# Graph kernel: three quarters of each source one-hot made by a compare and a multiply, with two numbers per partition

## The reference

```python
x = x + filter(h, src, dst)          # three hops of sums over edges, by node degrees
x = x + gat(h, edge_index, ...)      # attention over the edges, softmax by dst
x = x + relational(h, ..., edge_type, edge_weight, W1..W3)   # three rounds
x = x + attention(h, edge_attr_64, ...)
```

```python
scaled = feat * d_invsqrt
agg = segment_sum(scaled[src], dst, num_segments=3125)
```

## Time and profile before

| | |
|---|---|
| median of 3 runs | 6393.17 us (6391.6 to 6401.1) |
| profiled execution, its own time | 6387.14 us |
| its span, first to last instruction | 6385.3 us |
| PE busy | 4142.3 us, 65% |
| DVE busy | 3184.7 us, 50% |
| POOL busy | 3315.9 us, 52% |
| scatter, line 440 | 784 transfers, 874.8 us busy |
| hot_src, line 901 | 245 instructions, 263.5 us busy |
| hot_dst, line 903 | 245 instructions, 60.3 us busy |
| matmuls of the counting, line 975 | 1715, 385.0 us busy |

### The profile page before, as it was taken

One profiled execution on the slowest core, in us unless ns is written; L12 is line 12 of the kernel. 1 busy time (PEld: TensorE's weight loads), 2 busy tenths in 40 slices (PEclk: granted clock), 3 DMA queues, 4 the chain that ended last, 5 costly groups with the idle time before them and its releaser, 6 DMA issues. The chain is left out here.

```text
span 6385.3 us, 88933 instructions
## 1 busy us (share of the span) xinstructions
PE 4142.3 (65%) x19143; PEld 2771.2 (43%) x19144; DVE 3184.7 (50%) x7069; ACT 793.1 (12%) x2439; POOL 3315.9 (52%) x3323
## 2 busy tenths in 40 slices
PE   6969970003899788778746668888888844444431
PEld 5844430001499744444435534445445433333331
DVE  6966650005899456565566761122122255545556
ACT  1210000000110022222220010010010012222210
POOL 0048887772000077777733006737747547777761
PEclk7569985556899889898979979989999865555555
DMA  4311120001367577777745546767677643333331
GB/s 121 102 56 32 42 53 2 2 2 58 136 239 263 174 199 216 209 216 214 216 139 163 153 155 239 238 226 251 228 237 244 196 132 81 81 82 82 81 85 52
DMA packets 516122, 909.59 MB, mean 142 GB/s; under 512 B 100755, under 2 KB 349832, under 8 KB 476628
## 3 DMA queue, kind: packets, MB, share of 16 engines
q1 hardware_dynamic: 410094, 741.27, 35.7%
q0 software_dynamic: 105824, 165.90, 11.4%
HBM read 680.21 MB, written 226.65 MB: 142 GB/s over the span
## 5 line engine op out<-in xcount | busy, mean ns | idle before, releaser
L2768 POOL DMA_INDIRECT l_gathered<-l_table,l_st x816 | 775.6, 951 | 855.3 <-issue 782.0
L440 POOL DMA_INDIRECT by_src<-src_rec,src_pos x784 | 874.8, 1116 | 560.0 <-ACT attr_turned L742 321.2
L1790 POOL DMA_INDIRECT l_edges_by_src<-l_by_src,l_edges_st x816 | 786.7, 964 | 727.3 <-SPq L1884 478.9
L1790 POOL DMA_INDIRECT l_edges_by_src<-l_q,l_edges_st x816 | 778.4, 954 | 347.4 <-issue 242.9
L2837 PE MATMUL psum<-l_blocks,l_rows 128*128 128x512 f32 (+1 forms) x2016 | 814.7, 565 | 2.3 <-ACT l_rows L2779 2.3
L1869 PE MATMUL psum<-l_rows,l_edges_hot_t 128*128 x1632 | 443.1, 453 | 565.9 <-DVE l_scores L2907 542.6
L1688 PE MATMUL psum<-pair_hot_weight,pair_hot_dst 128*128 128x512 f32 x1200 | 642.9, 678 | 176.4 <-DVE pair_hot_dst L1678 165.6
L2796 DVE TENSOR_SCALAR l_hot<-iota,l_loc,l_weight 128x128 f32<-128x128 f32 x816 | 223.0, 360 | 916.8 <-PE psum L2853 913.6
L1869 PEld LDWEIGHTS psum<-l_rows,l_edges_hot_t 128*128 128x128 f32 x1632 | 379.0, 330 | 634.3 <-issue 634.3
L2837 PEld LDWEIGHTS psum<-l_blocks,l_rows 128*128 128x128 f32 x2016 | 373.5, 199 | 417.1 <-issue 412.3
L2504 PE MATMUL psum<-l_scaled,l_counts 128*128 128x128 f32 x3750 | 424.2, 277 | 18.8 <-ACT l_scaled L2429 18.8
(11 more groups left out here) (483 smaller groups left out, 5454.8 us busy)
## 6 DMA issues: line engine op xcount, KB each, us to landing
l_blocks<-pair_blocks SPq DMA_DIRECT2D x216, 1024.0 KB, 5.2
l_counts<-counts SPq DMA_DIRECT2D x65, 1600.0 KB, 6.8
pair_blocks<-pair_block SPq DMA_DIRECT2D x75, 1024.0 KB
l_edges_loc<-loc_by_tile SPq DMA_DIRECT2D x416, 128.0 KB, 3.0
l_rows<-l_edges_by_src SPq DMA_DIRECT2D x204, 256.0 KB
l_sum_rows<-l_rows SPq DMA_DIRECT2D x204, 256.0 KB, 2.6
attr_then_counts<-in_edge_attr SPq DMA_DIRECT2D x14, 1568.0 KB
counts<-attr_then_counts SPq DMA_DIRECT2D x13, 1600.0 KB
```

Of the source, the lines that this page charges most:

```text
L440: pool.indirect_dma_start(table, bass.IndirectOffsetOnAxis(ap=pos[:, e:e + 1], axis=0), rec[:, e, :], None).then_inc(s_out[g % R], 16)
L1790: pool.indirect_dma_start(a[:, r, g, :], None, table_src, bass.IndirectOffsetOnAxis(ap=st[:, r, g:g + 1], axis=0))\
L2768: pool.indirect_dma_start(sent[:, p, g, :], None, by_type, bass.IndirectOffsetOnAxis(ap=st[:, p, g:g + 1], axis=0))\
```

## The change

In `one_hots` the one instruction that wrote 3200 columns of `hot_src` becomes two. The first writes columns 0 to 2431 (19 of the 25 windows) by `is_equal` with the source number and then `mult` with a second number per partition, which is a column of ones. The second writes the other 768 columns by `is_equal` alone, as before. What stands in `hot_src` is the same. `hot_dst` is as it was. Each of the three instructions adds one to `s_hot`, so PE waits for three a visit.

```diff
+    WEIGHED = 19 * P
...
-            v.tensor_scalar(hot_src[:, bass.ds(place, 1), 0:NP].rearrange("p a c -> p (a c)"), iota[:, :],
-                            shifted[:, 0, bass.ds(t, 1)], None, ALU.is_equal).then_inc(s_hot, 1)
+            for cols, one in ((slice(0, WEIGHED), k.ones[:, 0:1]), (slice(WEIGHED, NP), None)):
+                v.tensor_scalar(hot_src[:, bass.ds(place, 1), cols].rearrange("p a c -> p (a c)"), iota[:, cols],
+                                shifted[:, 0, bass.ds(t, 1)], one, ALU.is_equal,
+                                *((ALU.mult,) if one is not None else ())).then_inc(s_hot, 1)
...
-                    pe.wait_ge(s_hot, (t + b) * 2 + 2)
+                    pe.wait_ge(s_hot, (t + b) * 3 + 3)
```

## The result

The changed kernel takes 6327.56 us (median of 4 runs, 6321.92 to 6332.13) against 6394.44 us for the kernel before (median of 4 runs, beside it). The ratio is 0.9894, with a 95% interval of 0.9876 to 0.9911: about 67 us faster. The forecast was 6313, with a range of 6270 to 6341 that also takes in the rival case two.

A forecast was written before the change was run, and what follows sets the result against it. POOL's scatter was taken to end the block, with the counting 560 us to spare. Missing scatters fall from 98 to 39 (quick 2, middle 9, slow 28), 74 us off 6387.1: 6313, own range 6295 to 6341, wider range 6270 to 6341.

The forecast's parts named there:

- case two: Two-number hot_src runs slower and leaves POOL alone: 6285 us at slow rate (chance 0.25), 6277 at half rate (0.10).
- The ceiling of 122 to 124 us: Scatter on POOL beside the counting: 97 transfers missing, 122 us lost, 124 over the whole line; the most that can be won.
- The rate of the two-number instruction: hot_src on DVE: 0.263 ns a column kept, so 0.91 us for 2432 columns and 0.41 for 768; other bound 1.04 ns.
- four: Two-number hot_src at half rate, 1.56 us, holds POOL out throughout: 40 more scatters missing, 6437 us; chance 0.12.
- Case three: Short holds catch the scatters that the long one lets go; rhythms stay, nothing moves: 6387 us; chance 0.10.
- The two requests and the holds: Each scatter asks twice, 0.46 to 0.71 us apart; an earlier end of the long hold lets the second request slip through.
- middle rhythm: hot_src starts 1.3 to 1.6 us apart; a scatter takes two visits, 2.74 us; change makes it one; missing 53 to 9.
- What I credited to the second number: Its extra 59 ns on hot_src delays the next long hold's start to 1.61 us, letting the second request through.
- The sum: Scatters missing over quick, middle and slow rhythms: 39 instead of 98, so 74 us less, 6313 us.
- quick: Window's start, hot_src starts 1.12 to 1.14 us apart, two visits a scatter; becomes one visit of 1.31; missing 17 to 2.
- slow rhythm: hot_src starts 1.6 to 1.7 us apart, one scatter a visit before and after; missing 28, unchanged.
- a mere shift: Everything behind the block should only be shifted in time.

The follow-up runs named there:

- the gap in the iota: Kernel before with the iota kept as 25 rows of 128 with a gap of two, hot_src still one uncut one-number instruction: 6268.66 us, ratio 0.9801.
- the summing compare: Changed kernel with the 2432 columns written by a one-number compare that also sums its answers, 768 by plain compare: 6274.9 us, ratio 0.981.
- the moved cuts: One-number split of hot_src cut elsewhere, against before: 1664 + 1536 columns 6311.11 us; 2816 + 384 6370.69 us; 3072 + 128 6398.47 us.
- the uncut kernel: All 3200 columns of hot_src in one two-number compare and multiply, against the kernel before: 6404.62 us, ratio 1.0004.
- the halves: hot_src in two plain one-number compares of 1664 and 1536 columns, against the kernel before: 6311.11 us, ratio 0.9869.
- the two kernels without holds: Long hot_src in a form that doesn't hold POOL out: gapped iota rows, 6268.66 us; 2432 columns by compare with sum, 6274.9 us.

## Why the prediction was right

**What bounds.** In the two profiled executions the block's end moved by exactly what the last scatter moved by, 66.1 us, with DVE idle for 504 us ahead of it. The ceiling of 122 to 124 us was right: the two kernels whose long instruction doesn't hold POOL out win 121 and 123 us at the last scatter.

**The rate of the two-number instruction.** Forecast 0.91 and 0.41 us at 0.263 ns a column, with four times that as the other bound. Measured 0.92 (median, 0.905 the least) and 0.410. Both rival cases two and four needed a slower rate, and fell with it. Case three, in which nothing moves, fell by the 361 scatters where there had been 310. As ideas the lower rates were sound: case two, with no hold, is what the gap in the iota and the summing compare made on purpose, at 6269 and 6275 us where it had said 6277 and 6285. Its price had a slip: 379.7 + 999 is 1379, not 1382. And its condition that PE might stay at 1.2 GHz did not come true: between 419 and 1302 us, where the summing compare sets the pace, the granted clock was 0.95 of full speed.

**The two requests and the holds.** Right in mechanism: one scatter a visit in the middle rhythm, 2.4 us scatters gone, and the time between the long hold's end and the next one decides, as the moved cuts show. I placed the second request between 0.46 and 0.71 us after the first; scatter by scatter it comes at 0.46 to 0.49, at the short end of that, so that the cut at 19 windows had about 0.06 us to spare with one number and 0.11 with two (a distance of 0.40 against 0.34 and 0.28).

**What I credited to the second number was wrong in weight.** The prediction let the extra 59 ns move the next hold's start and counted on it for the margin (1.61 against 1.52). The later start is there: the boundary lies 0.06 us lower with two numbers. But in the uncut kernel the instruction also ends 0.06 later, and the two cancel; in the cut one it is room that is not needed, since the split without the second number does as well. The forecast's total did not depend on it.

**The sum.** Forecast 39 scatters missing, last one near 1419, 6313 us. Measured 46, 1427.1 and 6327.6. Here are the terms, with the scatters that start between one long hot_src and the next, by how far apart these start:

| starts of hot_src apart | before: visits, missing | forecast missing | after: visits, missing |
|---|---|---|---|
| up to 1.60 us (quick and middle) | 132, 65 | 11 | 153, 16 |
| 1.60 to 1.70 (slow) | 89, 24 | 28 | 68, 22 |
| longer (changes of window, and others) | 24, 9 | nothing | 24, 8 |

Two terms were too small. The forecast kept the quick and middle rhythms at 1.31 and 1.37 us a visit, as though the counting stayed hidden behind PE. That step failed in part: 132 visits of the changed kernel last 1.35 to 1.60 us, 1.41 in the mean, and 126 of them follow without idle time on DVE, where 2 of 86 did before. DVE's forecast visit of 1.31 us became 1.41 since POOL, let in, holds DVE back in turn (1.01 us instead of 0.92 in the rows above). And the forecast let nothing be missing at the changes of window, though 9 are before. Its count of 98 for the kernel before fitted the 97 of the windows because it had the other terms too large by as much (70 and 28 for 65 and 24), which is luck. The slow rhythm, 6 fewer than forecast, took back about half of what these two left out. What remains is 7 scatters more than forecast, 9 us, which is the 8 us between 1419 and 1427.

**What lies behind the block.** I forecast a mere shift. From the last scatter to the span's end there are 4892.1 us before and 4903.2 after, 11 more in the profiled pair. This is not the change's: the same distance is 4904.0 in the split without the second number, 4905.9 with the second number alone, 4900.4 in the halves, 4886.0 and 4895.4 in the two kernels without holds. Of the 11 us of this pair, 11 lie in the relational layer, between its first and last gather:

```profile
L2768 POOL DMA_INDIRECT l_gathered<-l_table,l_st x816: 938/944/1066, 3834.4 to 5068.3; - x164
```

before, and after

```profile
L2771 POOL DMA_INDIRECT l_gathered<-l_table,l_st x816: 938/944/1056, 3768.9 to 5013.8; - x164
```

1233.9 and 1244.9 us. Over the ten traces, of kernels that are alike there, this stretch takes 1229.6 to 1249.0 us; what moves it was not tried. So the profiled pair differs by 55 us, the 66.1 of the block less these 11. By medians the gain is 67 us, close to the 66.1 of the block's end, and the forecast's 74 is too large by about the 8 us of its sum. With 20 us between the shortest and the longest of these distances behind the block, the closeness of the medians is in part luck.

## What to carry to other kernels

Where POOL issues indirect transfers beside vector work, look in the timeline for transfers that end a fixed time after a vector instruction (0.82 and 0.12 us here): the vector instruction's length at the top rate is then a price paid by the other engine. If the vector side has slack, give up its rate by layout rather than by tricks in the operation: one tile with a gap in its rows won 130 us where the cut and the multiply won 67. (The 130 and 67 are by medians, each against the runs of before beside it; at the last scatter they are 123 and 66.) And when an edit has two parts, run each alone before believing in either; here the part that gave the change its name did nothing for the time.

## What was not expected of the hardware

A fast instruction that holds POOL out can be made less harmful by cutting it: 1664 + 1536 columns take longer on DVE than 3200 and let 64 more scatters through in 513 us (374 against 310). Whether a scatter costs one visit or two turns on about 0.02 us: before, all 57 at a distance of up to 0.322 us were caught and all 93 from 0.338 on slipped through.

The blocking is mutual. In the changed kernel the 118 long hot_src that start about 0.4 us before a scatter's end take 1.01 us in the mean, nearly all others 0.92; in the kernel before it is seen too, in the slow rhythm (1.16 us in the earlier trace rows). In the halves hot_dst grows from 0.25 to 0.34 in the mean:

```profile
L906 DVE TENSOR_SCALAR hot_dst<-count_iota,tile_shifted x245 | 82.9, 339 | 0.0
```
